# A graph network's edge stage on four engines: code written out group by group, or held in hardware loops

## The reference

```python
row, col = src, dst                                # edge_index = stack([src, dst])
h = silu(edge_attr_8 @ W1 + b1)                    # (E, 8) -> (E, 128)
weights = h @ W2 + b2                              # (E, 128)
messages = node_feats[col] * weights               # gather x at the destination, multiply
aggregated = segment_sum(messages, row, N)         # sum by source
combined = concat([node_feats @ Wself + bself, aggregated])
x = layernorm(x + combined @ Wcat + bcat)
# second layer: means over neighbours in both directions, a GRU cell, again a layernorm
```

## Time and profile before

| | |
|---|---|
| time, median of 3 runs | 7326.63 us (7322.02 to 7331.11) |
| the profiled execution's own time | 7326.63 us |
| its span | 7324.5 us |
| first and last scatter start | 144.7 and 2316.1 us |
| TensorE clock granted, mean | 0.723 |
| bytes moved | 713.54 MB |

### The profile page before, as it was taken

How to read it: one execution, slowest core, us unless ns; L and a number is a source line. 1 busy time by engine, 2 the same in 40 slices (tenths; PEclk the granted TensorE clock), 3 DMA queues, 4 the chain that set the end, 5 groups by cost and what they waited for, 6 DMA issues and landing times.

```text
span 7324.5 us, 117378 instructions
## 1 busy us (share of the span) xinstructions
PE 4654.8 (64%) x25826; PEld 4002.3 (55%) x25826; DVE 3935.6 (54%) x9767; ACT 1862.8 (25%) x6476; POOL 5168.8 (71%) x5753
## 2 busy tenths in 40 slices
PE   5999999999997888333334433333555555555548
PEld 4888787877887888333333433332444444444434
DVE  7777777777776778433333533333433333333339
ACT  2333333333331001311111111111222222222218
POOL 2777777777776554677777777777777777777761
PEclk8778878787887999655665565665766766676769
DMA  3333333333335876222222222222333333333225
GB/s 111 123 119 121 119 121 119 120 120 121 120 120 153 228 231 205 78 54 54 54 54 54 51 54 54 54 53 54 74 70 72 72 70 72 72 71 72 71 79 181
DMA packets 947672, 713.54 MB, mean 97 GB/s; under 512 B 602499, under 2 KB 811606, under 8 KB 946622
## 3 DMA queue, kind: packets, MB, share of 16 engines
q0 software_dynamic: 163632, 347.28, 16.3%
q1 hardware_dynamic: 245634, 251.14, 11.5%
q10 hardware_dynamic: 538001, 110.77, 7.9%
HBM read 544.79 MB, written 170.29 MB: 98 GB/s over the span
## 4 chain that ended last, share of the span: by engine, by line
POOL 41%; issue 14%; PE 7%; DVE 2%; ACT 1%; DVEq 1%; DMA 1%; POOLq 0%; ACTq 0%; SPq 0%
POOL arena L757 41%; PE bank L1876 6%; PE bank L1922 1%; DVEq L405 1%; ACT acc_a L939 0%; DMA arena<-x1d,edge 0%; ACT acc_b L939 0%; DMA edge<-dlist 0%; DVE acc_a L1439 0%; DVE arena L1644 0%; DVE arena L1652 0%; POOLq L85 0%; DVE some_mv L1459 0%; DVE arena L1656 0%; DVE arena L1649 0%
## 5 line engine op out<-in xcount | busy, mean ns | idle before, releaser
L757 POOL DMA_INDIRECT arena<-x1d,edge x3322 | 3153.6, 949 | 1016.4 <-issue 1006.1
L1922 PE MATMUL bank<-arena 128*128 x7040 | 1566.8, 411 | 2260.4 <-SPq L579 1563.6
L1922 PEld LDWEIGHTS bank<-arena 128*128 128x128 f32 x7040 | 1454.0, 315 | 2397.9 <-issue 2397.1
L697 POOL DMA_INDIRECT msgs<-arena x1664 | 1642.0, 987 | 656.0 <-issue 496.6
L1568 DVE TENSOR_TENSOR arena<-bank,arena 128x1024 f32<-128x1024 f32 x440 | 538.4, 1224 | 2122.4 <-PE bank L1922 2050.6
L983 ACT ACTIVATE arena<-edge,arena 128x1 f32 x3520 | 677.5, 280 | 2035.8 <-issue 2001.6
L1833 PE MATMUL bank<-w2s,acc_b 128*128 128x128 f32 x3328 | 688.9, 371 | 0.0
L1833 PEld LDWEIGHTS bank<-w2s,acc_b 128*128 128x128 f32 x3328 | 585.7, 265 | 127.3 <-issue 127.3
L1574 DVE TENSOR_TENSOR acc_b<-acc_b,bank 128x129 f32 x1760 | 507.2, 288 | 207.6 <-DVE acc_b L1574 6.8
L1574 DVE TENSOR_TENSOR acc_a<-acc_a,bank 128x129 f32 x1760 | 507.3, 288 | 205.0 <-PE bank L1922 2.7
L1876 PE MATMUL bank<-arena 128*128 128x128 f32 x3712 | 499.1, 300 | 93.3 <-DVE acc_a L1439 64.8
(11 more groups left out here) (310 smaller groups left out, 4558.3 us busy)
## 6 DMA issues: line engine op xcount, KB each, us to landing
arena<-rows SPq DMA_DIRECT2D x208, 512.0 KB
arena<-msgs ACTq DMA_DIRECT2D x464, 136.0 KB, 3.2
arena<-msgs SPq DMA_DIRECT2D x464, 136.0 KB, 3.0
arena<-x1d,edge POOLq DMA_INDIRECT x3322
msgs<-arena POOLq DMA_INDIRECT x1664
pred<-arena ACTq DMA_DIRECT2D x98, 256.0 KB
arena<-pred SPq DMA_DIRECT2D x12, 1792.0 KB, 8.9
arena<-xwin SPq DMA_DIRECT2D x208, 64.0 KB, 1.8
```

The source lines that it names most:

```text
L697: pool.indirect_dma_start(msgs, bass.IndirectOffsetOnAxis(ap=pos[:, b, j:j + 1], axis=0), mrow[:, b, j, :], None).then_inc(scattered[b], 16)
L757: pool.indirect_dma_start(grow_t[:, sl, 0:D], None, x1d, bass.IndirectOffsetOnAxis(ap=edge2[:, odd * RING + sl, 1:2].bitcast(i32), axis=0) ...
L1922: last = mm(sum_at(q, k), oh1[:, q % 2, k, :], grow[:, bass.ds(rows_at[q * TG + k], CW)], start=True, stop=True)
```

## The change

On four engines the edge stage's Python loop over rounds becomes hardware loops: on POOL all 104 rounds; on PE and ACT round 0 by itself, a loop over rounds 1 to 98 (with the self term's block), a loop over 99 to 102, and round 103 by itself; on DVE round 0, a loop over rounds 1 to 101, and two rounds by themselves. SP's code stays. What is computed, the tiles, the buffers and the order of the work on each engine stay too.

```diff
-            for it in range(NG // 2):
+            with pool.Fori(0, NG // 2) as it:
                 scatters(it)
...
-            for it in range(NG // 2):
-                edge_group(it, more=it < NG // 2 - 1, nb=it - 1 if 1 <= it <= NB else None)
+            edge_group(0)
+            with act.Fori(1, NB + 1) as it:
+                edge_group(it, nb=it - 1)
+            with act.Fori(NB + 1, NG // 2 - 1) as it:
+                edge_group(it)
+            edge_group(NG // 2 - 1, more=False)
...
-            for it in range(NG // 2):
-                edge_group(it, more=min(2, NG // 2 - 1 - it))
+            edge_group(0)
+            lead, per = ls.n, 2 * 8
+            with dve.Fori(1, NG // 2 - 2) as it:
+                ls.loop(it - 1, per)
+                ls.n = lead
+                edge_group(it)
+            ls.n, ls.it = lead + per * (NG // 2 - 3), None
+            edge_group(NG // 2 - 2, more=1)
+            edge_group(NG // 2 - 1, more=0)
...
-            for it in range(NG // 2):
-                edge_group(it, more=it < NG // 2 - 1, nb=it - 1 if 1 <= it <= NB else None)
+            edge_group(0)
+            with pe.Fori(1, NB + 1) as it:
+                edge_group(it, nb=it - 1)
+            with pe.Fori(NB + 1, NG // 2 - 1) as it:
+                edge_group(it)
+            edge_group(NG // 2 - 1, more=False)
```

## The result

The changed kernel took 7386.4 us (median of 4 runs, 7372.75 to 7392.63), the kernel before 7328.2 us beside it (4 runs, 7322.02 to 7331.11). The ratio is 1.0101, with a 95% interval from 1.0081 to 1.0121. The forecast was 7326 us, its own range 7316 to 7338, and the range that was to hold 8 in 10 went from 7300 to 7348. The measured time lies outside both.

What follows compares the result with a forecast made beforehand. The prediction took POOL's scatters to bound the edge stage, with PE 0.37 us per group behind. All terms were 0, so 7326.6 us + 0 gave 7326 us, own range 7316 to 7338, 8 in 10 within 7300 to 7348.

Steps and rivals of the forecast that it cites:

- POOL at 10.33 us per group sets the pace, PE has 0.37 us to spare: Edge stage: POOL's scatters and own gaps bound it, 2150 us over 208 groups; PE is the second limit.
- The stalls stay: Edge stage, POOL: 14 stalls, mostly 1.85 us, at every 112th scatter remain in the loop; no gain counted.
- rival A: Edge stage, POOL: the stalls belong to straight code and go, 23 us gained, 7303 us; chance 0.16.
- PE's register work costs nothing: Edge stage, PE: 18 register instructions and a jump per trip, covered by queued matmuls; 0, fully exposed 0.44 us per group.
- POOL's too: Edge stage, POOL: five register instructions and a jump per trip cost 0; about 27 us if all exposed.
- Instruction traffic is on no path, jumps load nothing: Edge stage: instruction packets on q8 and q14, 0.5% of DMA engines' time, vanish; 0 us. Looped code is not loaded again.
- rival C: Edge stage, PE: each jump loads code again, 1.2 us per group beyond the spare, 245 us, 7572 us; chance 0.02.
- ACT and DVE: Edge stage: 24 and 26 register instructions per trip, mostly covered; at most 0.15 us per group on PE's round trip, taken as 0.
- A constant clock: Edge stage, PE: tacit; the sum has no term for a change in matmul time or clock.
- Rival B: Edge stage: register work of PE, ACT and DVE lands on PE's path, 0.22 us per group, 46 us, 7372 us; chance 0.14.

Runs made afterwards that it cites:

- e2: e1 plus the whole change, hardware loops on all four engines, against the kernel before: 7395.96 us, ratio 1.0097.
- e12: e1 without new loops, plus one unread ACT copy ahead of L870 in the first half of rounds 1 to 98: 7343.41 us, ratio 1.0028 to the kernel before.
- e13: e1 with ACT and PE in loops, DVE and POOL written out: 7364.83 us, ratio 1.0057 to the kernel before.
- e1: The kernel before with two PE register instructions per turn added in the last gather stage, edge stage untouched: 7326.83 us, ratio 0.9999.
- e10: e1 with PE, DVE and POOL in loops, ACT written out: 7318.2 us, ratio 0.9994 to the kernel before.
- e16: e2 with ACT's jump moved behind the key columns and L892's DMA behind the next round's first-half key columns: 7321.03 us, ratio 0.9999 to the kernel before.
- e17: e2 with L892's DMA moved behind the next round's first-half key columns, ACT's jump left in place: 7332.37 us, ratio 0.9998 to the kernel before.
- e11: e2 with ACT's trip turned so its jump stands behind the key columns, L892's DMA left in place: 7320.26 us, ratio 0.9996 to the kernel before.
- e18: e12's one extra ACT copy together with DVE's loop, ACT written out: 7338.98 us, ratio 1.0007 to the kernel before.
- e15: e1 without new loops, plus two unread ACT copies ahead of L870 in the first half of rounds 1 to 98: 7354.42 us, ratio 1.004 to the kernel before.
- e9: e1 with ACT alone in loops, the other three engines written out: 7366.27 us, ratio 1.0063 to the kernel before.
- e14: e1 with ACT and DVE in loops, PE and POOL written out: 7398.71 us, ratio 1.0107 to the kernel before.
- e3: e1 with PE alone in loops, the other three engines written out: 7324.86 us, ratio 0.9996 to the kernel before.
- e4: e1 with DVE alone in a loop, the other three engines written out: 7327.42 us, ratio 0.9997 to the kernel before.
- e6: e1 with POOL alone in loops: ratio 1.0017 to the kernel before, which itself took 8981 us in that comparison.

## Why the prediction was wrong

**The sum that decides.** From the window row and the wait for L858 a chain of PE can be added up: busy time plus that wait, per group. The rest of a group is PE's wait for `pos`, which is where POOL's pace shows (0.37 us per group before, 0.12 in e2), and at most 0.07 us of others. The table thus splits the time; it does not by itself say what caused what. Busy time, wait, matmul and group are of the one profiled execution from 400 to 2200 us, the ratio is of all executions: e12's profiled one was its fastest (7335.53 us), e13's its slowest (7376.29).

| kernel | busy + wait = chain, us per group | ns per matmul | us per group | ratio |
|---|---|---|---|---|
| before | 9.74 + 0.33 = 10.07 | 157.1 | 10.46 | 1 |
| e1, same edge stage | 9.86 + 0.28 = 10.13 | 159.1 | 10.43 | 0.9999 |
| e10, all but ACT | 9.90 + 0.19 = 10.09 | 159.6 | 10.42 | 0.9994 |
| e16, jump and DMA moved | 9.91 + 0.20 = 10.10 | 159.9 | 10.44 | 0.9999 |
| e17, DMA moved | 9.89 + 0.22 = 10.11 | 159.3 | 10.44 | 0.9998 |
| e11, jump moved | 9.69 + 0.47 = 10.15 | 156.0 | 10.43 | 0.9996 |
| e18, copy, DVE's loop | 9.76 + 0.51 = 10.27 | 157.4 | 10.47 | 1.0007 |
| e12, one copy | 9.97 + 0.37 = 10.34 | 160.6 | 10.50 | 1.0028 |
| e15, two copies | 9.85 + 0.59 = 10.44 | 159.0 | 10.56 | 1.0040 |
| e9, ACT | 9.98 + 0.53 = 10.51 | 160.9 | 10.67 | 1.0063 |
| e13, ACT and PE | 10.03 + 0.49 = 10.52 | 161.7 | 10.69 | 1.0057 |
| e14, ACT and DVE | 10.15 + 0.49 = 10.63 | 163.9 | 10.79 | 1.0107 |
| e2, all loops | 10.19 + 0.48 = 10.67 | 164.2 | 10.82 | 1.0097 |

Sums are of unrounded terms; e3 and e4 lie at 10.15 and 10.17 with 10.42 and 10.45 per group. Up to about 10.3 us the group takes 10.42 to 10.47 whatever PE does: POOL's pace. Beyond, it takes the chain plus 0.12 to 0.17. The chain has two terms, and e11 and e2 differ in one only: the wait is the same (0.47 and 0.48), the matmuls take 156.0 and 164.2 ns. The wait alone sorts nothing: it is 0.51 in e18, which loses nothing, 0.59 in e15 and 0.48 in e2.

**Point by point.**

- *POOL at 10.33 us per group sets the pace, PE has 0.37 us to spare.* Right for the kernel before, though e1's trace, of the same stage, has 0.29. e9's chain uses it up, and e11's, at 10.15, does not.
- *The stalls stay (against rival A).* Right: 14 in the trace of every kernel here, straight or looped. That they are of constant length, its argument against A, is only roughly so (see the last section).
- *PE's register work costs nothing.* Right where POOL sets the pace (e3) and beside ACT's loop (e13 against e9). *POOL's too* (e6, e10).
- *Instruction traffic is on no path, jumps load nothing (against rival C).* Right: e2 has no instruction packet from 400 to 2200 us, and its 83 jumps on PE there take 207 or 208 ns each. By the rule that the prediction quoted from the Trainium skill ("Runtime: NRT & Kernel Launch", section "Instruction fetch mechanics") the loops should fit, and the trace agrees.
- *ACT and DVE: "Only those right before L858 and L870, L1347 and L1394 are on PE's round trip, some 4 x 0.04 = 0.15 us per group at the very most. I take 0, since both engines wait for PE or for scatters anyway."* This is the step that failed, in three ways. The bound counted the durations of four instructions; measured, one place alone has 0.49 us per trip (0.24 per group): in e2's trace the register instructions behind L858 last 29 to 59 ns but start 60 to 100 ns apart, and 0.16 us pass from the jump's start to the next one's. I looked for cover ("behind an instruction of 0.2 to 1.3 us that covers them") without asking whether the instruction right ahead lets the sequencer run on: L892's DMA doesn't. And ACT's 580.7 us of idle time at L886 were taken as proof that it had time, while its first-half sequence L858, L870, L864, L858 had none: PE already waited 57.4 us for it. That row stands beside those of the earlier trace rows, and I did not use it.
- *A constant clock.* The sum left PE's matmuls at their 157.1 ns. In e2 they take 164.2, and 10,324 / 166.4 = 62 of them per group make 0.44 us, the larger term beside the 0.15 us by which the wait grew. Against e1, the same code as e2 but for the loops, they are 0.32 and 0.20 us. Rival B had the right direction and nearly the size (7372 us), but by luck: 0.44 of its 0.59 us per group were PE's own register work, which costs nothing, and it left the clock as it was too.

**What stays open.** Why the clock falls. The runs show that it stays at 0.79 to 0.81 where ACT's head is shortened (e11, e16, e17) and at 0.76 in e2 and e14, and that DVE's loop moves it only together with ACT's (e14, not e4 or e18). A changed phase between PE's waits and its two clock levels may do this; no run tested it. So where the loss comes from is shown (ACT's jump behind L892's issue, with DVE's loop beside it), and how it becomes 69 us is shown for the smaller term only. Nor was shown where the rest of ACT's register work adds to e9, which costs 42 us with a shorter delay at L870 than the two copies' 32.

No variant beats both kernels: e10 (0.9994), e11, e16 and e17 can't be told from the kernel before, since POOL sets the pace in all of them. e11 or e17 keep the loops without the loss.

## What to carry to other kernels

When code goes into a hardware loop, look at each engine for the place where its sequencer cannot run ahead: behind a DMA or a wait that needs the engine's own last result. A jump and a few register instructions cost nothing while the engine's own work still runs (e17), and held ACT up by 0.35 us behind such a place (0.44 us from the issue to L870 in e2, 0.09 before); choose the start of the trip so that the jump falls where the engine waits long. And ask of an engine with much idle time which of its sequences another engine waits for: its longest wait says nothing about its tightest. Where another engine's loop moves PE's clock, as here, the loss can be larger than the delay.

## What the runs showed of the hardware

POOL has a stall at every 112th scatter: in all kernels here, always behind 113, 225, 337 and so on to 1,569 scatters, whether or not POOL has waited for others in between. In the kernel before 11 of the 14 last 1.85 to 1.87 us (the others 2.21, 2.37 and 2.99), in e2 8 last 2.23 and the rest 1.67 to 1.85, and in e6 all 14 last 2.23; what they are is open. One of them, in e2's timeline, one scatter after a wait for messages:

```profile
1050.13 0.97 POOL L697 DMA_INDIRECT msgs<-arena  x1 [2.26 <-DVE arena L1379]
1053.33 0.97 POOL L697 DMA_INDIRECT msgs<-arena  x1 [2.23 <-issue]
```

The same matmuls in the same order took 156.0 ns each in e11 and 164.2 in e2 (mean granted clock 0.81 and 0.76). The two kernels differ only in where ACT's jump and the register instructions with it stand; two traces of one code differed by 2 ns.
